# One masked maximum a unit from the fifth unit on, and three chunks finished behind the last weights, in a two-layer graph network on one Trainium2 core

## What is computed

```
def _L1_gnn_ref(indices, features, ...):
    h_att = features @ Watt_w + Watt_b
    e = leaky_relu(h_att[src] @ a1 + h_att[dst] @ a2, 0.2)
    e = e - max(e)
    exp_e = exp(e)
    alpha = exp_e / (segment_sum(exp_e, dst)[dst] + 1e-09)
    h_neigh = segment_sum((features @ W1_w + W1_b)[src] * alpha, dst)
    return leaky_relu(features + h_neigh + (features * h_neigh) @ W2_w + W2_b, 0.2)
x = layernorm(x + _L0_gnn_ref(...))
x = layernorm(x + _L1_gnn_ref(edge_index, x, ...))
```

## Time and profile before

| what | us |
|---|---|
| median of 3 runs (lowest, highest) | 1375.3 (1372.75, 1376.11) |
| the profiled execution: its time, its span | 1371.59, 1369.6 |
| VectorE busy over the span | 1182.4 (86%) |
| TensorE busy over the span | 1155.7 (84%) |
| ScalarE, GpSimd busy over the span | 917.4 (67%), 873.8 (64%) |

### The profile page before, as it was taken

The page is one execution under the profiler, slowest core; times in us unless marked ns, Lnnn a source line. Parts: engine busy times, 40 slices in busy tenths (PEclk is TensorE's granted clock), DMA queues, the critical chain, the costliest instruction groups (busy, mean ns, idle before and its releaser), DMA issues. The chain is left out here.

```text
span 1369.6 us, 27977 instructions
## 1 busy us (share of the span) xinstructions
PE 1155.7 (84%) x8980; PEld 938.9 (69%) x9072; DVE 1182.4 (86%) x2186; ACT 917.4 (67%) x2210; POOL 873.8 (64%) x945
## 2 busy tenths in 40 slices
PE   5786787798899977899978999999999595888995
PEld 4543455457778756788766877777777494888995
DVE  7798976649899978899978999999998668999976
ACT  2564675568788987698977888788877134544523
POOL 3377777777777777777777777777777501334511
PEclk9697998899999999999999999999999898879998
DMA  8232342266899478899698988999898785678761
GB/s 258 76 98 82 87 132 80 78 161 173 236 258 255 155 232 220 233 252 244 193 270 225 280 237 231 245 286 239 246 260 222 198 227 174 202 232 268 267 212 38
DMA packets 246565, 276.09 MB, mean 202 GB/s; under 512 B 35079, under 2 KB 194470, under 8 KB 243078
## 3 DMA queue, kind: packets, MB, share of 16 engines
q1 hardware_dynamic: 197762, 183.84, 45.7%
q0 software_dynamic: 25792, 53.29, 12.3%
q10 hardware_dynamic: 22852, 37.02, 12.3%
HBM read 162.85 MB, written 111.20 MB: 200 GB/s over the span
## 5 line engine op out<-in xcount | busy, mean ns | idle before, releaser
L1977 POOL DMA_INDIRECT edge_rows<-x_rows,pos x806 | 778.8, 966 | 250.5 <-issue 229.5
L1475 ACT ACTIVATE h_edge<-ps_wh,w_col 128x128 f32<-128x128 f32 x808 | 229.3, 367 | 105.9 <-PE ps_wh L1276 98.8
L1320 PEld LDWEIGHTS ps_d<-back_one,back 128*128 128x128 f32 x1914 | 232.1, 193 | 61.4 <-issue 57.8
L1320 PE MATMUL ps_d<-back_one,back 128*128 128x128 f32 x1914 | 241.2, 278 | 4.7 <-DVE agg_t L1794 4.2
L1283 PE MATMUL ps_wh<-wf,filt 128*128 128x128 f32 x1616 | 233.5, 289 | 0.6 <-DVE filt L1577 0.5
L1269 PE MATMUL ps_v<-f_t,wf 128*128 128x512 f32 x400 | 223.1, 641 | 0.0
L1581 DVE TENSOR_TENSOR x_rows<-ps_wh,h_edge 128x512 f32<-128x512 f32 x202 | 137.9, 683 | 86.2 <-DMA edge_rows<-x_rows,pos 45.3
L1283 PEld LDWEIGHTS ps_wh<-wf,filt 128*128 128x128 f32 x1616 | 204.1, 198 | 2.6 <-DVE filt L1577 2.6
L1112 PE MATMUL ps_wh<-yard 128*128 128x150 bf16 x1575 | 138.0, 233 | 61.6 <-DVE yard L1102 39.8
L1112 PEld LDWEIGHTS ps_wh<-yard 128*128 128x128 bf16 x1575 | 108.7, 100 | 107.1 <-DVE yard L1102 84.3
L2470 PE MATMUL ps_wh<-loan,yard 128*126 128x129 f32 x1250 | 154.5, 288 | 26.0 <-DVE yard L2756 15.3
(11 more groups left out here) (354 smaller groups left out, 1423.6 us busy)
## 6 DMA issues: line engine op xcount, KB each, us to landing
c_tab<-yard SPq DMA_DIRECT2D x25, 1575.0 KB
yard<-c_tab SPq DMA_DIRECT2D x25, 1575.0 KB, 6.7
dst_bc<-dst ACTq DMA_DIRECT2D x99, 252.0 KB
back<-edge_rows SPq DMA_DIRECT2D x42, 516.0 KB, 9.3
edge_rows<-x_rows,pos POOLq DMA_INDIRECT x806
back<-edge_rows SPq DMA_DIRECT2D x48, 258.0 KB, 5.1
m_tab<-yard SPq DMA_DIRECT2D x25, 393.8 KB
mask_room<-m_tab SPq DMA_DIRECT2D x5, 1968.8 KB, 12.9
```

The source lines that it names most:

```text
L1320: mm = nc.tensor.matmul(acc(c), back_rows(n)[:, k0 + t, 0:D], back_one[:, m % 2, o + t, :], start=t == 0, stop=t == k1 - k0 - 1, skip_grou ...
L1475: copy = nc.scalar.activation(h_edge[:, j, q, :], ps_wh[:, bank, 1, q * D:(q + 1) * D], ACT.Copy, scale=w_col[:, t(q)])
L1977: return pool.indirect_dma_start(table[s], bass.IndirectOffsetOnAxis(places_here, 0), rows, None)
```

## The change

`TWICE` goes from 8 to 4. The table `BESTS` then asks for two maxima a unit in units 0 to 3 and one a unit from unit 4 on, and all 25 are done ahead of unit 19 (`TOP_AT`), not 15. Candidates, largest score, bias and eps come four units later, and `FROM` is 22. The dictionaries are written anew: a chunk is averaged at each of the steps 22 to 25, mixed one step later, finished two steps later, and the loops of TensorE, ScalarE and VectorE run over `STEPS` = 27 steps, of which the last two have no unit. In the last step chunk 4's average and rest stand ahead of the finish of chunk 2 and the mix of chunk 3. On TensorE chunk 4's turn goes ahead of chunk 3's output; on ScalarE eps is made behind the last `larger`, and chunk 2's rows are normalised behind the last two slopes. The number of instructions on each engine is the same.

```
-TWICE = 8
+TWICE = 4
...
-            AVERAGE_AT = {FROM: 0, FROM + 1: 1, FROM + 2: 2, FROM + 4: 3}
-            MIX_AT = {FROM + 1: 0, FROM + 2: 1, FROM + 3: 2, FROM + 5: 3}
-            FINISH_AT = {FROM + 2: 0, FROM + 3: 1, FROM + 4: 2, FROM + 6: 3}
-            MIX_LAST = max(MIX_AT)
+            SHARED = (NC - 1) * HB
+            AVERAGE_AT = {FROM + c: c for c in range(NC - 1)}
+            MIX_AT = {FROM + 1 + c: c for c in range(NC - 1)}
+            FINISH_AT = {FROM + 2 + c: c for c in range(NC - 2)}
+            STEPS = FROM + NC
...
-                    if n in MIX_AT and n < MIX_LAST:
+                    if n in MIX_AT and n < STEPS - 1:
                         output(MIX_AT[n])
                     if n in AVERAGE_AT:
                         turn_back(AVERAGE_AT[n])
-                output(NC - 2)
                 pe.wait_ge(inv_done, 2 * NC + 1)
                 turn_back(NC - 1)
+                output(NC - 2)
                 output(NC - 1)
...
-                for n in range(FROM, len(UNITS)):
-                    if n - 1 in MIX_AT and n - 1 < MIX_LAST:
+                for n in range(FROM, STEPS):
+                    if n - 1 in MIX_AT:
                         slope(MIX_AT[n - 1])
...
+                    if n == STEPS - 1:
+                        divided(NC - 1)
+                    if n in FINISH_AT:
                         inverse_deviation(act, mv2, FINISH_AT[n], stats_done, rough, NC)
-                divided(NC - 1)
                 slope(NC - 2)
                 slope(NC - 1)
+                normal(NC - 3).then_inc(norm_done, 1)
                 inverse_deviation(act, mv2, NC - 2, stats_done, rough, NC)
...
-                for n in range(len(UNITS)):
-                    weights(n)
+                for n in range(STEPS):
+                    if n < len(UNITS):
+                        weights(n)
...
-                    if n in FINISH_AT and FINISH_AT[n] < NC - 2:
+                    if n == STEPS - 1:
+                        average(NC - 1)
+                        divided_rest(NC - 1)
+                    if n in FINISH_AT:
                         finish_rows(FINISH_AT[n])
                     if n in MIX_AT:
                         mix(MIX_AT[n])
-                average(NC - 1)
-                divided_rest(NC - 1)
                 mix(NC - 1)
```

More of the change, by code:

```diff
@@ L2201, in build @@
             FROM = TOP_AT + 3
-            AVERAGE_AT = {FROM: 0, FROM + 1: 1, FROM + 2: 2, FROM + 4: 3}
-            MIX_AT = {FROM + 1: 0, FROM + 2: 1, FROM + 3: 2, FROM + 5: 3}
-            FINISH_AT = {FROM + 2: 0, FROM + 3: 1, FROM + 4: 2, FROM + 6: 3}
-            MIX_LAST = max(MIX_AT)
+            SHARED = (NC - 1) * HB
[3 more added lines that the diff above has]
+            STEPS = FROM + NC
+            assert SHARED <= FROM and STEPS >= len(UNITS)
             ACT_DIVIDES, ACT_FIRST, ACT_LAST = 3, 2, 2
             GM_S1, GM_MAX, GM_EPS = 3, 12, 16
-            SHARED = (NC - 1) * HB
             POOL_K = 2
@@ L2457, in _, with unit_sums @@
                 spread_top(s1_all[:], GM_S1 + 2)
-                for n, (c, h) in enumerate(UNITS):
+                def unit_sums(n):
+                    c, h = UNITS[n]
                     if c == 0:
@@ L2473, in _ @@
                     mm.then_inc(a_used, 1)
+                for n in range(STEPS):
+                    if n < len(UNITS):
+                        unit_sums(n)
                     if n == 3:
@@ L2618, in _ @@
                         keep(c - 1)
[L2619 to L2623, removed]
-                for n in range(FROM, len(UNITS)):
-                    if n - 1 in MIX_AT and n - 1 < MIX_LAST:
+                act.wait_ge(hop, 3)
+                act.wait_ge(gm, GM_EPS)
+                nc.scalar.activation(eps_raw[:], ps_v[0:Q, 1, 256:256 + NB], ACT.Exp, bias=eps_bias[0:Q, 0:1],
+                                     scale=-1.0).then_inc(eps_made, 1)
+                for n in range(FROM, STEPS):
+                    if n - 1 in MIX_AT:
                         slope(MIX_AT[n - 1])
```

## The result

The changed kernel took 1380.3 us (median of 5 runs, 1379.55 to 1380.42) against 1375.3: a ratio of 1.0039, with a 95% interval of 1.0028 to 1.0050. That is 5.0 us or 0.4% slower; 1380.3 had been forecast. Of the runs of all kernels in this document one, of e1_fill_both, took 1517.2 us at a mean granted clock of 0.733, and it is left out of that kernel's ratio.

What follows compares the result with a forecast made beforehand. VectorE bounds the units with two maxima, TensorE the work behind them. The gain of 16 us is taken back by the chain: +0.3 at full clock plus 4.7 for the clock makes +5.0 on 1375.3, 1380.3 us; whole range 1373.5 to 1384.5.

Steps and rivals of the forecast that it cites:

- The maxima: VectorE's maxima stage: 15 one-maximum units at 6.32 us put unit 19's weights at 1295.2; candidates take 1.3 us.
- TensorE until turn 2: TensorE from unit 19's sums: 39.9 us of work to 1336.0, last unit's sums ending at 1333.2 instead of 1349.6.
- The chain: Mix, output, slope and finish after the last sums, across engines: 7.1 us a round; full-clock sum -0.2 to +0.5, carried +0.3.
- less than one is left: At mix 4 on VectorE: half the mix done at 1352.2, old mix starting at 1352.5; of 16 us under one remains.
- The clock: TensorE behind two new pauses of 4.3 and 5.4 us: matmuls at half clock cost 4.7 us together.
- the upper bound: All matmuls left on TensorE after the pauses run at half clock, costing another 7.7 us.
- the signs named: Unit 19's weights near 1295, sums ending near 1333, two TensorE gaps over 4 us, clock 0.50, outputs over 4 us.
- ScalarE: End of the tail: normalising chunk 2 (2.0 us) precedes chunk 3's deviation, GpSimd refines in 1.9, last refinement starts at 1361.1.
- no fall: Rival: TensorE's clock does not fall, or the fall finds no matmuls; +0.3 us, or +2 with one fall; chance 0.25.
- The overlap: Rival: two chunks' finishing rounds overlap at VectorE's rate, 4.7 us a chunk, giving 1370.3 us; chance 0.10, with any shorter chain.
- The pace: Rival: loads or GpSimd's products cannot follow one-maximum units; four units cost 13.6 us more, 1389 and above; chance 0.05.

Runs made afterwards that it cites:

- e1_fill_both: The changed kernel with 13 useless matmuls in TensorE's pause ahead of output 2 and 20 ahead of turn 4; ratio to before 0.9995.
- e4_mix_first: The changed kernel with each mix ahead of the previous chunk's finish on VectorE, outputs waiting only for that finish's first operation; ratio to before 0.9995.
- e7_best_no_fill: The changed kernel with TWICE = 5, mixes ahead of finishes, shorter output waits, chunk 4's division and chunk 3's deviation ahead of normalising; ratio to before 0.9977.

## Why the prediction was right

The time came out as forecast, by the mechanism that was forecast: a chain that takes the gain back, and the slow clock on top. That it came out to the tenth is luck, since some terms were off and cancel. Term by term:

- **The maxima.** Unit 19's weights were put 94.8 us behind unit 4's; measured 95.0. Loads and GpSimd kept the pace of 6.3 us. The candidates took 1.5 where 1.3 was taken.
- **TensorE until turn 2.** The last unit's sums were to end 172.8 us behind unit 0's weights (1333.2 - 1160.4); it was 173.3. The gain of 16 us is 15.9.
- **The chain.** +0.3 us at full clock was the sum, -0.2 to +0.5 its bounds. The kernel with both pauses filled, which has the chain and not the slow clock, has a tail longer by 0.5 and a ratio of 0.9995. Two errors cancel in this. By the prediction's own steps mix 4 starts at 1351.4, 191.0 us behind unit 0's weights and 1.1 earlier than before; its "less than one is left" sets the end of half that mix against the old mix's start. In e1_fill_both mix 4 starts at 192.0, where it started before (192.1): nothing is left. Half of this microsecond comes from the sums' end, half from the steps behind it. The way from mix 4 to the last refinement was in turn 0.5 shorter than worked out, as the term of ScalarE says. The wait that was argued from VectorE's list (mix behind finish) is shown by e4_mix_first, where it is taken away and the pauses shrink from 4.25 and 5.51 us to 2.51 and 2.95.
- **The clock.** 2.7 us were taken for the first burst and 1.7 to 2 for the second, 4.7 together; 2.4 and 2.1 were measured, 4.5. The choice near the lower end was right because the clock came back before the last output: had it stayed low, as the upper bound had it, some 2 us more would have gone there, by an estimate from the halves at either clock (2.3 us and 1.26). Of the signs named one came only in part: output 3 took 3.95 us and not over 4. The rule of the Trainium skill's page "TensorE: Matmul & The Clock Gate", section "Why this matters for your kernels", that pauses between bursts are to be avoided, agrees with both pauses here (4.25 and 5.51 us, 0.50 behind each).
- **ScalarE.** From mix 4 to the last refinement 9.7 us were worked out (1351.4 to 1361.1), against 8.6 before, so that the normalising costs 1.1; measured 9.2, a cost of 0.6. The mis-sized term is the refinement on GpSimd, taken at 1.9 us as in the kernel before. It took 1.4, because its operation of 0.69 us took 0.20.
- **The rivals.** The clock fell, so that "no fall" is out; its time, 0.3 us over before, lies within the interval of e1_fill_both, where the fall is taken away. The overlap could not happen by the list, and with a list that lets it happen it did, but it was worth less than the 1370.3 us worked out for it: e4_mix_first gives back the loss (0.9995) and stays some 4 us above that time. The pace held.

What carries the loss is thus the clock: without its 4.5 us what is left is the 0.5 of the tail in e1_fill_both, whose ratio shows no measurable change. The gain of 15.9 us, in turn, is taken back by the chain.

## What to carry to other kernels

When work is moved out of the way of one engine, ask where the steps that were hidden beside it go: here the last weights came 16 us earlier, and a chain of mix, output, slope and finish, some 8 us a round even at full clock (7.65 from mix 2 to mix 3 in e1_fill_both), took all of it back, because in one engine's list each mix stood behind the finish of the chunk before. Such a round is read from the rows of before, step by step, and the list says what may overlap. And price what is left on TensorE at both levels of its clock: behind a pause of 4.25 us half an output, which takes 1.1 us from start to start, took 2.3, and matmuls of no use laid into the pauses, where TensorE waits for others anyway, gave that back at no cost that shows.

## What the runs showed of the hardware

The start of unit 0's weights, behind the same instructions in all nine kernels, varied by 4.9 us between profiled executions (1160.4 to 1165.3), as much as the change itself is worth; the tails measured from there agree with the ratios to 1.2 us, and to 1.5 in e7_best_no_fill.

The length of a pause on TensorE did not settle here whether the clock fell. Pauses of 1.1 us in e1_fill_both and of 2.37 us in e7_best_no_fill left it at 1.00, and those of 2.51 and 2.95 us in e4_mix_first were followed by 0.50. The pause ahead of unit 3's sums is 2.17 us in the kernel before and in the kernel after: before, the unit ran at full clock in 5.74 us, and after, the clock fell to 0.50 behind the pause and the unit took 7.41.

Small operations of VectorE and GpSimd took longer beside each other: two of the candidates' operations took 1.59 and 1.21 us beside GpSimd's products and 0.25 and 0.19 without, and GpSimd's L2084 took 0.69 us beside an addition of two tensors on VectorE and 0.20 beside its statistics.
